# A selective scan with the channel halves as its outer loop, and the normalisation and output product of an image made in the steps of the scan

## What is computed

```python
delta = softplus(dt_out + dbias)              # per image, order, channel, pixel
xc = exp(delta * A) * xc + delta * u * B      # the scan, one pixel after another
y = xc * C + u * D                            # summed over the four orders
...
yz = y * zf                                   # zf = silu(z)
mu = yz.mean(-1, keepdims=True)               # over the 256 channels
xc = yz - mu
var = (xc * xc).mean(-1, keepdims=True)
yn = gamma * xc / jnp.sqrt(var + 1e-05) + beta
out = yn @ Wout
```

## Time and profile before

| | us |
|---|---|
| median of 3 runs (4614.57 to 4617.05) | 4614.59 |
| the profiled execution | 4611.34 |
| its span, first to last instruction | 4609.5 |
| TensorE busy in the span | 3873.8 (84%) |
| VectorE busy | 3406.9 (74%) |
| ScalarE busy | 2678.2 (58%) |
| GpSimd busy | 1391.3 (30%) |
| DMA, mean over the span | 75 GB/s |

### The profile page before, as it was taken

The page is one execution under the profiler, slowest core; times in us unless marked ns, Lnnn a source line. Parts: engine busy times, 40 slices in busy tenths (PEclk is TensorE's granted clock), DMA queues, the critical chain, the costliest instruction groups (busy, mean ns, idle before and its releaser), DMA issues. The chain is left out here.

```text
span 4609.5 us, 73934 instructions
## 1 busy us (share of the span) xinstructions
PE 3873.8 (84%) x25590; PEld 2996.1 (65%) x25590; DVE 3406.9 (74%) x7889; ACT 2678.2 (58%) x6018; POOL 1391.3 (30%) x1373
## 2 busy tenths in 40 slices
PE   6888887799999999999999999676999644455579
PEld 4666665699988998899888998444666311111148
DVE  4666666577787777777787777695666798899934
ACT  3666665577776777767776667333222466666621
POOL 2434443100010000200010000112244599999910
PEclk9999999799999999999999999898999755555579
DMA  7777774200010000100010000212222311122143
GB/s 205 204 199 198 197 198 137 76 24 21 18 37 27 20 24 16 42 24 24 17 39 13 10 10 10 67 62 95 77 77 71 145 55 55 60 69 71 58 151 102
DMA packets 274687, 346.40 MB, mean 75 GB/s; under 512 B 34954, under 2 KB 159754, under 8 KB 272778
## 3 DMA queue, kind: packets, MB, share of 16 engines
q1 hardware_dynamic: 261738, 320.55, 22.8%
q0 software_dynamic: 12288, 16.92, 1.4%
q10 hardware_dynamic: 288, 4.19, 0.2%
HBM read 209.58 MB, written 130.02 MB: 74 GB/s over the span
## 5 line engine op out<-in xcount | busy, mean ns | idle before, releaser
L864 ACT ACTIVATE l_ph<-l_T 128x512 fp32r<-128x512 f32 x1024 | 612.4, 598 | 547.2 <-PE l_T L777 547.2
L974 DVE TENSOR_TENSOR l_pl<-l_T,l_ph 128x512 fp32r<-128x512 f32 x1024 | 707.3, 691 | 274.9 <-ACT l_ph L864 274.2
L963 DVE CUSTOM_DVE_ANT_0 l_pr<-l_S,l_zero 128x512 f32<-128x512 f32 x1024 | 704.7, 689 | 74.1 <-PE l_S L700 11.2
L869 ACT ACTIVATE l_pr<-l_pr,l_st 128x512 f32<-128x512 f32 x1024 | 731.5, 714 | 1.1 <-DVE l_st L969 1.0
L789 PE MATMUL l_O<-l_ph,l_vh 128*128 128x256 f32 x2048 | 661.7, 323 | 12.2 <-DVE l_pl L974 12.1
L777 PE MATMUL l_T<-l_ident,l_pr 128*128 128x128 f32 x4096 | 612.8, 272 | 0.0
L777 PEld LDWEIGHTS l_T<-l_ident,l_pr 128*128 128x128 f32 x4096 | 507.6, 140 | 136.2
L790 PE MATMUL l_O<-l_ph,l_vl 128*128 128x256 f32 x2048 | 577.9, 282 | 0.0
L791 PE MATMUL l_O<-l_pl,l_vh 128*128 128x256 f32 x2048 | 576.8, 282 | 0.0
L1005 POOL TENSOR_TENSOR l_xs<-l_xs,l_bob 128x128 f32<-128x128 f32 x128 | 57.1, 461 | 1644.7 <-DMA l_xs<-x 1643.6
L1658 PE MATMUL l3b_C<-l_D,l_sel 32*128 32x512 f32 x256 | 216.4, 845 | 384.5 <-DVE l3b_E L1716 384.1
(11 more groups left out here) (241 smaller groups left out, 8842.7 us busy)
## 6 DMA issues: line engine op xcount, KB each, us to landing
hls<-l_hl SPq DMA_DIRECT2D x64, 512.0 KB, 4.7
l_qs<-hls SPq DMA_DIRECT2D x96, 256.0 KB, 3.8
l_ks<-hls SPq DMA_DIRECT2D x96, 256.0 KB, 4.0
l_xc<-x1t SPq DMA_DIRECT2D x64, 256.0 KB, 2.7
zs<-l3a_tmp SPq DMA_DIRECT2D x64, 256.0 KB, 2.0
l3b_z<-zs SPq DMA_DIRECT2D x64, 256.0 KB, 2.8
yz<-l3b_z SPq DMA_DIRECT2D x64, 256.0 KB, 2.0
l3c_y<-yz SPq DMA_DIRECT2D x16, 1024.0 KB, 17.1
```

The costliest lines, as they stand in the source:

```text
L864: e.activation(ph[:, i, :], psT[:, i, :], ACT.Copy).then_inc(p_hi, 1)
L869: e.activation(pr[:, s, es], pr[:, s, es], ACT.Exp, bias=st[:, s, 9:10], scale=SC, accum_out=st[:, s, 10 + k:11 + k]).then_inc(exped, 1)
L963: e.tensor_tensor_reduce(pr[:, s, ks], psS[:, bk, :], zero[:].broadcast_to([128, 512]), 1.0, -3.0e38, ALU.add, ALU.max, st[:, s, kc:kc + 1 ...
L974: e.tensor_tensor(pl[:, i, :], psT[:, i, :], f32(ph[:, i, :]), ALU.subtract).then_inc(p_lo, 1)
```

## The change

- **Order of the units.** `unit(m)` = (h, n, a4, c): first half 0 of all four images, then half 1. The plane is k = 4h + n. Half 1 of u is no longer kept for all images: `X1` takes image 0, and the planes of `U0` are refilled from `ub1` once half 0 no longer needs them (`plane`, and the loads at T = 105, 113, 121).
- **`yz`** keeps only half 0. A chunk of half 1 stays in SBUF after its gate, in `y[:, c, 1, :]`, and half 0 of the same chunk is loaded beside it.
- **`finish3` is gone**; its work for chunk f of image n stands in `scan` at four steps from t = 32k + 40 + 4c (k = 4 + n): `squares` at t and t+1, `sums` at t+2, `products` at t+3. The loop is longer: `times` goes to M + 45, so that the last image's chunks come after the last unit.
- **The mean is folded into weights.** Instead of mean, subtraction and product there are `cen` = identity minus 1/256 (and -1/256 for the other half), by which TensorE makes one centred half at a time into the single bank psF for ScalarE's Square; and `gc` = gamma Wout less its column mean, by which the product is taken of the uncentred y. These and `bw` are made once, at T = 12 (`PREPARE`).
- **1/sigma** comes from Ln and Exp with scale -0.5 on ScalarE, for four columns of a chunk at a time.
- **Banks.** psd has 2 instead of 3; psF is new; psX serves the gates and the products in turn, ordered by `X_use` and `X_free`. psF is ordered by `F_use` and `F_free`.

The diff, cut to its core (the removed `finish3` and renamed waits are left out):

```diff
-def scan(nc, io, zs, yz, ub1, skip, K):
+def scan(nc, io, zs, yz, ub1, skip, out, K):
...
-        U1 = P.sb("u1", [128, NI, TOK])
+        X1 = P.sb("u1", [128, TOK])
...
+        y = P.sb("y", [128, 8, 2, 512])
+        wo, gw, gc = P.sb("wo", [128, 2, 128]), P.sb("gw", [128, 2, 128]), P.sb("gc", [128, 2, 128])
+        mean, cen, bw = P.sb("mean", [128, 128]), P.sb("cen", [128, 2, 128]), P.sb("bw", [128, 128])
+        cg, rs = P.sb("cg", [128, 5]), P.sb("rs", [128, 2, 2, 4])
+        sq, os = P.sb("sq", [128, 2, 512]), P.sb("os", [128, 2, 512])
+        psd = P.ps("d", [128, 2, 512])
+        psF = P.ps("F", [128, 512])
...
-            return m // 64, m // 32 % 2, m // 8 % 4, m % 8
-
-
-
-        fetches, gates = {}, {}
+            return m // 128, m // 32 % 4, m // 8 % 4, m % 8
+        def plane(h, a4):
+            if h == 0:
+                return U0[:, a4, :]
+            return U0[:, a4 - 1, :] if a4 else X1[:]
...
+                if k >= NI:
+                    f, t = 8 * (k - NI) + c, 32 * k + 40 + 4 * c
+                    squares[t], squares[t + 1] = (f, 0), (f, 1)
+                    sums[t + 2] = f
+                    products[t + 3] = f
+        PREPARE = 12
+        times = range(M + 45)
...
+            e.dma_start(X1[:], ub1[0]).then_inc(u_in[0], 16)
+            for dst, src in ((ident[:], io["ident"]), (cg[:, 0:2], io["L3_conv_gamma"].rearrange("(h p) -> p h", p=128)),
+                             (cg[:, 2:4], io["L3_conv_beta"].rearrange("(h p) -> p h", p=128)), (wo[:], io["L3_conv_Wout"].rearrange("(h p) d -> p h d", p=128))):
+                e.dma_start(dst, src, allow_slow_non_contiguous=True).then_inc(weights, 16)
+            for h in range(2):
+                w.wait_ge(skip_out[h], 16)
+            e.dma_start(acc[:, 1, :], skip[0]).then_inc(acc_in[1], 16)
...
+                    n, sl = k % 4, slice(512 * c, 512 * c + 512)
+                    if 1 <= k <= NI:
+                        w.wait_ge(y_out[c], 16 * k)
+                    elif k > NI:
+                        w.wait_ge(X_full, X_use["out", 8 * (k - NI - 1) + c] + 1)
+                    e.dma_start(y[:, c, 1, :], zs[n, k // 4, :, sl]).then_inc(z_in[c], 16)
+                    if k >= NI:
+                        e.dma_start(y[:, c, 0, :], yz[n, :, sl]).then_inc(y_in[c], 16)
...
+                    w.wait_ge(X_free, X_use["gate", (k, c)] + 1)
+                    if k < NI:
+                        e.dma_start(yz[k, :, 512 * c:512 * c + 512], y[:, c, 1, :]).then_inc(y_out[c], 16)
...
+                if T - 2 >= 96 and (T - 2) % 8 == 7 and (T - 2) // 8 - 12 < 3:
+                    a = (T - 2) // 8 - 12
+                    w.wait_ge(dued, T - 1)
+                    e.dma_start(U0[:, a, :], ub1[a + 1]).then_inc(u_in[a + 1], 16)
+                if T in products:
+                    f = products[T]
+                    n, c = divmod(f, 8)
+                    w.wait_ge(X_free, X_use["out", f] + 1)
+                    e.dma_start(out[n, 8 * c:8 * c + 8].rearrange("(t r) c d -> (r c) t d", r=2), os[:, f % 2, :].rearrange("p (t c) -> p t c", t=4)).then_inc(o_out[f % 2], 16)
...
-                    if T >= 3:
-                        w.wait_ge(soft, T - 2)
-                    e.matmul(psd[:, T % 3, :], dtw[rows, 256 * a4 + 128 * h:256 * a4 + 128 * h + 128], part(D[rows, :], a4, c), start=True, stop=True).then_inc(d_full, 1)
+                    if T >= 2:
+                        w.wait_ge(soft, T - 1)
+                    e.matmul(psd[:, T % 2, :], dtw[rows, 256 * a4 + 128 * h:256 * a4 + 128 * h + 128], part(D[rows, :], a4, c), start=True, stop=True).then_inc(d_full, 1)
...
+                    u = X_use["gate", (k, c)]
+                    w.wait_ge(weights, 64)
                     w.wait_ge(added, 32 * k + 32)
-                    if j:
-                        w.wait_ge(gated, j)
-                    e.matmul(psX[:], ident[:], part(acc[:, k % 2, :], k // 2, c), start=True, stop=True).then_inc(X_full, 1)
+                    if u:
+                        w.wait_ge(X_free, u)
+                    e.matmul(psX[:], ident[:], part(acc[:, k % 2, :], k % 4, c), start=True, stop=True).then_inc(X_full, 1)
+                if T in products:
+                    f = products[T]
+                    u, c = X_use["out", f], f % 8
+                    w.wait_ge(X_free, u)
+                    w.wait_ge(prepared, 8)
+                    for j in range(4):
+                        for h in range(2):
+                            t = e.matmul(psX[:, 128 * j:128 * j + 128], y[:, c, h, 128 * j:128 * j + 128], gc[:, h, :], start=(h == 0), stop=(h == 1))
+                    t.then_inc(X_full, 1)
+                if T in squares:
+                    f, h = squares[T]
+                    u, c = F_use["square", (f, h)], f % 8
+                    w.wait_ge(prepared, 8)
+                    w.wait_ge(X_free, X_use["gate", (NI + f // 8, c)] + 1)
+                    w.wait_ge(y_in[c], 16 * (f // 8 + 1))
+                    if u:
+                        w.wait_ge(F_free, u)
+                    e.matmul(psF[:], cen[:, h, :], y[:, c, 0, :], start=True, stop=False)
+                    e.matmul(psF[:], cen[:, 1 - h, :], y[:, c, 1, :], start=False, stop=True).then_inc(F_full, 1)
+                if T in sums:
+                    u = F_use["sum", sums[T]]
+                    w.wait_ge(F_free, u)
+                    for j in range(4):
+                        for h in range(2):
+                            t = e.matmul(psF[:, j:j + 1], sq[:, h, 128 * j:128 * j + 128], mean[:, 0:1], start=(h == 0), stop=(h == 1))
+                    t.then_inc(F_full, 1)
...
+                    e.activation(tE[:, T % 5, :], psd[:, T % 2, :], ACT.Exp).then_inc(raised, 1)
+                if T in squares:
+                    f, h = squares[T]
+                    u = F_use["square", (f, h)]
+                    w.wait_ge(F_full, u + 1)
+                    e.activation(sq[:, h, :], psF[:], ACT.Square).then_inc(F_free, 1)
+                if T in sums:
+                    f = sums[T]
+                    w.wait_ge(F_full, F_use["sum", f] + 1)
+                    if f >= 2:
+                        w.wait_ge(X_free, X_use["out", f - 2] + 1)
+                    e.activation(rs[:, f % 2, 0, :], psF[:, 0:4], ACT.Ln, bias=cg[:, 4:5]).then_inc(F_free, 1)
+                    w.wait_ge(F_free, F_use["sum", f] + 1)
+                    e.activation(rs[:, f % 2, 1, :], rs[:, f % 2, 0, :], ACT.Exp, scale=-0.5).then_inc(inv, 1)
...
+                if T == PREPARE:
+                    w.wait_ge(weights, 64)
+                    for h in range(2):
+                        e.tensor_scalar(gw[:, h, :], wo[:, h, :], cg[:, h:h + 1], None, ALU.mult).then_inc(prepared, 1)
+                    e.memset(mean[:], 1.0 / 256).then_inc(prepared, 1)
+                    e.memset(cg[:, 4:5], 1.0e-5).then_inc(prepared, 1)
+                    w.wait_ge(prepared, 3)
+                    e.tensor_scalar(cen[:, 1, :], mean[:], -1.0, None, ALU.mult).then_inc(prepared, 1)
+                    e.tensor_tensor(cen[:, 0, :], ident[:], mean[:], ALU.subtract).then_inc(prepared, 1)
+                    w.wait_ge(small_full, 1)
+                    for h in range(2):
+                        e.tensor_tensor(gc[:, h, :], gw[:, h, :], psF[:, 0:128], ALU.subtract).then_inc(prepared, 1)
+                    e.tensor_copy(bw[:], psF[:, 128:256]).then_inc(prepared, 1)
                 if T in gates:
                     k, c = gates[T]
-                    j = 8 * k + c
-                    w.wait_ge(z_in[j % 2], 16 * (j // 2 + 1))
-                    w.wait_ge(X_full, j + 1)
-                    e.tensor_tensor(tZ[:, j % 2, :], psX[:], tZ[:, j % 2, :], ALU.mult).then_inc(gated, 1)
+                    w.wait_ge(z_in[c], 16 * (k + 1))
+                    w.wait_ge(X_full, X_use["gate", (k, c)] + 1)
+                    e.tensor_tensor(y[:, c, 1, :], psX[:], y[:, c, 1, :], ALU.mult).then_inc(X_free, 1)
+                if T in products:
+                    f = products[T]
+                    w.wait_ge(X_full, X_use["out", f] + 1)
+                    w.wait_ge(inv, f + 1)
+                    w.wait_ge(prepared, 9)
+                    if f >= 2:
+                        w.wait_ge(o_out[f % 2], 16 * (f // 2))
+                    for j in range(4):
+                        t = e.scalar_tensor_tensor(os[:, f % 2, 128 * j:128 * j + 128], psX[:, 128 * j:128 * j + 128], rs[:, f % 2, 1, j:j + 1], bw[:],
+                                                   ALU.mult, ALU.add)
+                    t.then_inc(X_free, 1)
...
-    finish3(nc, io, yz, out)
+        scan(nc, io, zs, yz, ub1, skip, out, K)
```

(40 more changed lines are left out.)

183 lines of the change are left out of this document (23 added, 160 removed).

## The result

The changed kernel takes **4667.1 us** (median of 4 runs, 4661.8 to 4671.9) against 4615.8 for the kernel before in the same comparison: ratio 1.0109, 95% interval 1.0091 to 1.0127. It is 1.1% slower. Forecast were 4570 us and a range up to 4615. The profiled execution has a span of 4664.8 us, where my sum had 4565.5: 99 us are to be explained.

A forecast was written before the change was run, and what follows sets the result against it. TensorE was taken to bound the finishing stage, VectorE the scan, with GpSimd close behind. Preparation +3.6, steps +58.1, tail -122.7 and clock +17 gave -44 us, so 4570 us, range 4525 to 4615.

The forecast's parts named there:

- The clock: TensorE's clock during steps and tail: full with falls, 8% of the 218 us that half clock throughout would add, +17 us.
- the walk: Timing by engine at full clock: steps 168 to 258 take 323.7 us against 265.6, the tail 91.5 against 214.2.
- Order of units, banks, DMAs, queues: 0: Scan: reordered units, psd with two banks, plane refills and SP's new waits cost nothing; 3 us a gate if fetch lead is lost.
- Preparation 3.6: At T=12, making the weights with four more VectorE instructions of 0.29 adds 3.6 us on VectorE's path; bounds 0 and 6.
- Table loads: none: ScalarE alternates squares, Ln and Exp without reloading tables; if Square needed loads, they would cost 164 us.
- Quartets of 12.4 and 15.9 at full clock: Steps 168 to 259: four steps take 12.4 us without gates (12 quartets), 15.9 with gates (11); +58.1 us in all.
- Everything TensorE does costs twice as much at the half clock: Price rule for all TensorE work, from two instructions taking 2.08 us at half clock against 1.02 at full.
- The three stalls named: Quartets: VectorE waits 1.27 us behind the second square; gated t+3's product waits 2 us for psX; scalings wait for the product.
- A chunk of 8.9 in the tail, 10.9 with gates: After the scan, nine chunks run in sequence through psF, five at 8.9 us and four at 10.9; tail 91.5 us.
- Rival 1, the clock: Quartets' lean stretches: clock swings or stays low, 218 us times the half-clock share, giving 4620 to 4772 us; chance 0.14.
- the prediction's own sign for it: Stretch from T=168: the forecast is wrong if clock rows show more than a quarter of it at 0.50.
- The rule of the Trainium skill: TensorE in the quartets: small idle gaps between matmul groups alternating PSUM banks can swing the clock, giving rival 1's time.

The follow-up runs named there:

- x_wide: Changed kernel with variance sums as 4 instructions of 512 columns instead of 16 of one column (output scaled wrongly): 4598.4 us, 0.9975 of the kernel before.
- x_part: Changed kernel with squares, sums, products and scalings of the last image only; images 0 to 2 not normalised: 4511.5 us, 0.9785 of the kernel before.
- x_fill: Changed kernel plus two unread wide products between identity and output product in each step with both: 4645.2 us, 1.0071 of the kernel before.
- x_widefill: Changed kernel with wide sums (output scaled wrongly) and two unread products at the psX hand-over: 4588.6 us, 0.9951 of the kernel before.
- x_dr2: Changed kernel with ScalarE squaring y from SBUF into f32r, variance from sums without centred products, output product in psF: 4550.3 us, 0.9895 of the kernel before.

## Why the prediction was wrong

The failed step is the one headed **The clock**: "I take 8% of it, half of layer 2's share, since the gaps are shorter." It read the fall in layer 2 as the work of an idle gap, counted TensorE's busy time in the quartets, and found it enough. Measured were 60% of the steps and 30% of the tail. Its evidence for a clock that stays up was also cut off too early: in layer 2 it "stayed up" over 3017 to 3027, with 59% busy, but that window ends where the clock fell. TensorE had paused for 3.83 us until 3025.87, and the three microseconds behind the window show 0.52:

```profile
3027.00:3030.00 3.00, 3.00 (x5) 0.97 (x4) 2.97 (x9) 0.69 (x1) 0.53 (x1) 0.52 0.08 29
```

With the measured shares the prediction's own prices, 147 us for the clock in the steps (205 against 58) and 74 in the tail, give 323.7 + 0.60 x 147 = 412 and 91.5 + 0.30 x 74 = 114, where 405.3 and 116.4 were measured. (147 and 74 are 221; the prediction adds them up as 218.) That this comes out so near is luck: two errors cancel. The changed kernel and x_wide differ in the clock and in little else, so a line through both is an estimate of what each part costs. In the steps, 405.3 at a share of 0.60 and 362.3 at 0.20 give 341 us at full clock, and 107 for the clock. In the tail, 116.4 at 0.30 and 101.0 at 0 give 101, and 51. So the walk has the full clock 17 and 10 us too short, and the clock itself too dear by a third.

By this estimate the miss of 99 us is: 62 for the clock's share (64 + 15 us measured, less the 12 + 6 forecast; rounded), 27 for the walk at full clock, 10 in untouched layers.

Point by point:

- *Order of units, banks, DMAs, queues: 0.* Right within 2.9 us (x_part: 268.5 against 265.6).
- *Preparation 3.6.* It took 4.5 on VectorE; the start of T=168 moved by 3.2 beside the drift. Right in sum; see the last section for its parts.
- *Table loads: none.* Right; Square, Ln and Exp alternate and the profile lists no load among them.
- *Quartets of 12.4 and 15.9 at full clock.* In x_wide, with 80% at full, the quartets average 13.6 and 18.6. The mis-sized term is C and d, 0.73 and not 0.45, and 1.31 where they use the same rows. "Everything TensorE does costs twice as much at the half clock" fails for them too. The three stalls named (second square, psX, result of the product) are there.
- *A chunk of 8.9 in the tail, 10.9 with gates.* In x_wide it is 8.84 from F to F, but 12.4 with gates: four times 1.5 us, most of what the tail at full clock lacks.
- *Rival 1, the clock.* This is what happened, at 0.14, and the prediction's own sign for it, more than a quarter of the stretch at 0.50, was there. Its place, "the quartets' lean stretches", is only part of it: the clock fell also where TensorE had no pause. Its formula, 58.1 + 3.6 - 122.7 + 218 x 0.53, 0.53 being the share over steps and tail together, is +55, and the kernel is 51 us slower. That is closer than it deserves: 10 us of the profiled execution's 55 stand in untouched layers, and the two errors above cancel in it.
- *The argument for it that I had in hand.* In the scan before, the clock stood at 0.50 with TensorE 52% busy, and layer 2 at 0.92 with 70%. I compared 65 to 70% of my quartets with the latter. But layer 2's products have 128 rows; of my quartets' busy time two fifths were C, d and sums (1.8 + 1.7 of 8.8 us without gates, at the prediction's prices).
- *The rule of the Trainium skill* ("TensorE: Matmul & The Clock Gate", "A second HAM failure mode: psum-queue depth-cycling"), that small idle gaps between groups of matmuls make the clock swing: the swing is there, 0.60 of the steps, and filling one gap took it to 0.36 (x_fill). It isn't the whole of it, since the clock also fell behind six microseconds without a gap, in 5 of 22 falls.

What stays open: how narrow or low products weigh against wide ones. The runs show only that exchanging one form for another of the same duration moved the share by 0.4, that leaving it out moved nothing in the steps (in the tail the share went from 0.30 to 0.04), and that more wide work raised the clock. No kernel ran with C and d changed, so how much they and how much the waits keep the clock down is not separated.

## What to carry to other kernels

Before moving work to an engine that looks half idle, ask at which clock it is idle and what its new mixture will be: here a TensorE that was 90% busy, in part with one-column and 32-row products, was granted the half clock for 60% of the time, in which every f32 product of 128 rows took twice as long. Work out the move at both clocks, and if only one of them pays, treat the clock as the question and not as a surcharge. Look also at how far a window is cut off: a clock that "stays up" may fall right behind its end. Raising the clock alone made up for the loss and little more (x_widefill, 0.5% under the kernel before, with its sums in the wrong layout). What paid most was less TensorE work: squares from SBUF by ScalarE, f32r for sums whose rounding doesn't matter, one add on GpSimd, and no gate and product in one PSUM bank. These came in bundles, so what each is worth alone is not shown, except for the f32r sums of x_dr2 (41 us in the steps).

## What the runs showed of the hardware

- Clock by kind of work: the variance sums as 16 one-column products or as 4 of 512 columns occupy TensorE alike (1.81 and 1.83 us), and the share of the steps at half clock was 0.60 or 0.20. With no sums it was 0.60 too, but in the tail 0.04 instead of 0.30.
- Unread wide products made the kernel faster: two of them in 11 of the 91 steps shortened these by 13 us (x_fill).
- C and d, f32r of 32 rows and 512 columns, gain from the clock by an amount that depends on the order in which they read. In the orders 0 and 1, where the pixels lie side by side, one took 0.79 us at the half clock and 0.50 at the full one; in 2 and 3, where `part` steps from image row to image row, 0.90 and 0.80: hardly any gain. A pair held TensorE for 0.84 and 0.73 us if one of the two was of the second kind, and 0.43 at full clock if none was.
- Two such products on different rows started within 0.01 us of each other, in the quartets looked at; on the same rows the second started 0.72 us behind the first at half clock and 0.62 at full, and the pair held TensorE for 1.41 and 1.31 us (second kind of order).
- Two of VectorE's `tensor_scalar` instructions were four times as long beside a busy GpSimd. The preparation of the changed kernel, with GpSimd's two instructions there:

```profile
3685.45 1.51 DVE L1813 TENSOR_SCALAR l3b_gw<-l3b_wo,l3b_cg 128x128 f32<-128x128 f32 x2
3685.61 1.27 POOL L1855 TENSOR_TENSOR l_acc<-l_acc,l3b_E 128x512 f32<-128x512 f32 x1
3686.84 1.27 POOL L1865 TENSOR_TENSOR l3b_du<-l3b_E,l_u 128x512 f32<-128x512 f32 x1
3687.14 1.05 DVE L1817 TENSOR_SCALAR l3b_cen<-l3b_mean 128x128 f32<-128x128 f32 x1
3688.11 0.28 DVE L1818 TENSOR_TENSOR l3b_cen<-l3b_ident,l3b_mean 128x128 f32<-128x128 f32 x1
```

The first row holds two instructions. The first gw took 0.28 us, as in `finish3` with GpSimd idle (0.29); it began before GpSimd's add. The second took 1.32 us and ended at 3686.96, 0.08 behind that add; the first cen took 1.05 and ended at 3688.19, 0.08 behind GpSimd's next instruction. The `tensor_tensor` of 0.28 began when GpSimd had stopped, so it tells nothing of instructions with two sources. The kernels above show the same 0.28 and 1.32. That GpSimd shares VectorE's SBUF interfaces, with contention for VectorE instructions that run in a 2-port performance mode or have two SBUF inputs, is stated by the Trainium skill ("GPSIMD Engine Reference", "1. Specifications"). The slow ones here have one tensor as input, so the second cause is out; that they ran in such a mode is shown by no run here.
